# Value and key units in one block of every second round, the first key read between two clips

## What is computed

```python
lat = layer_norm(latents, ln_lat_g, ln_lat_b)      # latents: 4 x 256 x 128
ctx = layer_norm(context, ln_ctx_g, ln_ctx_b)      # context: 4 x 512 x 128
q = (lat @ Wq)                                     # 16 heads of 64
k, v = jnp.split(ctx @ Wkv, 2, axis=-1)
k = apply_rope(k, cos, sin)
attn = jnp.einsum('bhnd,bhsd->bhns', q, k) * scale
attn = jnp.clip(attn, -11.0, 11.0)
attn = jax.nn.softmax(attn, axis=-1)
out = jnp.einsum('bhns,bhsd->bhnd', attn, v)
return out @ Wo + bo
...
x = x + _L0_xattn_ref(_layernorm(x, axis=-1), ctx_1024, ...)
```

## Time and profile before

| | before |
|---|---|
| times | 425.7, 425.8 and 427.06 us, median 425.8 us |
| the profiled execution | 426.81 us, its span 424.9 us |
| PE busy | 402.7 us (95%) |
| DVE busy | 336.0 us (79%) |
| POOL busy | 257.5 us (61%) |
| ACT busy | 178.2 us (42%) |
| the rounds: S of round 0 to S of round 30 | 62.16 to 266.74 us |

### The profile page before, as it was taken

One profiled execution on the slowest core, in us unless ns is written; L12 is line 12 of the kernel. 1 busy time (PEld: TensorE's weight loads), 2 busy tenths in 40 slices (PEclk: granted clock), 3 DMA queues, 4 the chain that ended last, 5 costly groups with the idle time before them and its releaser, 6 DMA issues.

```text
span 424.9 us, 8269 instructions
## 1 busy us (share of the span) xinstructions
PE 402.7 (95%) x3040; PEld 296.0 (70%) x3040; DVE 336.0 (79%) x655; ACT 178.2 (42%) x282; POOL 257.5 (61%) x225
## 2 busy tenths in 40 slices
PE   3988799999999999999999998999999999999996
PEld 2666686667657776677766675687767788888884
DVE  8887759999989988998877997885778772655554
ACT  6867354545445245544263534336256443000000
POOL 6823549999998977998987686758335840000000
PEclk9999989999999999999999999999999999999999
DMA  7687422221211112111111162547347640000000
GB/s 181 160 214 105 89 66 61 52 81 44 51 44 32 38 37 52 26 45 43 40 37 39 41 110 65 137 69 153 54 107 155 148 64 2 6 13 8 6 6 14
DMA packets 84746, 28.63 MB, mean 67 GB/s; under 512 B 71957, under 2 KB 79050, under 8 KB 84706
## 3 DMA queue, kind: packets, MB, share of 16 engines
q1 hardware_dynamic: 81748, 26.80, 28.6%
q10 hardware_dynamic: 2958, 1.30, 1.4%
HBM read 17.67 MB, written 2.02 MB: 46 GB/s over the span
## 4 chain that ended last, share of the span: by engine, by line
PE 58%; DVE 31%; issue 4%; ACT 2%; DMA 2%; ACTq 1%; POOL 0%; DVEq 0%
PE psum L1230 7%; DVE rden L1638 7%; PE psum L1211 6%; DVE e_sb L1631 6%; PE psum L1414 5%; PE psum L1415 5%; PE psum L1413 5%; PE psum L1374 4%; PE psum L1376 4%; PE psum L1375 4%; PE psum L1249 3%; PE psum L1240 2%; DVE rope_b L1512 2%; DVE xn L1457 2%; DVE kT L1517 2%
## 5 line engine op out<-in xcount | busy, mean ns | idle before, releaser
L578 POOL TENSOR_TENSOR e_part<-e_sb 128x512 f32<-128x512 f32 x64 | 88.4, 1397 | 25.7 <-DVE e_sb L1631 25.7
L839 ACT ACTIVATE e_sb<-psum 128x1024 f32<-128x1024 f32 x64 | 62.3, 1023 | 81.4 <-PE psum L1211 78.5
L1631 DVE TENSOR_SCALAR e_sb<-e_sb 128x1024 f32<-128x1024 f32 x64 | 63.8, 1026 | 5.9 <-ACT e_sb L839 5.9
L1211 PE MATMUL psum<-q_t,kT 64*128 64x256 f32 x512 | 64.2, 389 | 0.0
L1230 PE MATMUL psum<-e_sb,v_sb 128*64 128x256 f32 x512 | 63.8, 386 | 0.0
L1638 DVE RECIPROCAL rden<-psum 128x256 f32<-128x256 f32 x32 | 55.9, 1747 | 9.1 <-PE psum L1240 9.1
L1840 DVE SCALAR_TENSOR_TENSOR x_sb<-psum,dw,x_sb 128x128 f32<-128x128 f32 x96 | 33.7, 351 | 37.1 <-PE psum L1415 34.5
L1211 PEld LDWEIGHTS psum<-q_t,kT 64*128 64x128 f32 x512 | 46.7, 186 | 13.9 <-issue 8.4
L1230 PEld LDWEIGHTS psum<-e_sb,v_sb 128*64 128x64 f32 x512 | 33.7, 136 | 22.3 <-issue 6.6
L607 POOL TENSOR_TENSOR xeT_lo<-xeT,xeT_hi 128x512 fp32r<-128x512 f32 x24 | 31.4, 1309 | 28.7 <-ACT xeT_hi L853 28.6
L570 POOL TENSOR_TENSOR kT<-kT,raw 128x512 f32<-128x512 f32 x32 | 44.2, 1382 | 2.7 <-DMA raw<-rope_b 1.9
(11 more groups left out here) (202 smaller groups left out, 733.3 us busy)
## 6 DMA issues: line engine op xcount, KB each, us to landing
raw<-rope_b SPq DMA_DIRECT2D x116, 64.0 KB, 2.0
w_raw<-in_L_ffn_W_dram SPq DMA_DIRECT2D x96, 64.0 KB, 2.3
gates<-gate_dram SPq DMA_DIRECT2D x6, 768.0 KB, 5.0
ctx_sb<-in_ctx_dram SPq DMA_DIRECT2D x4, 256.0 KB, 6.7
vbd<-v_dram SPq DMA_DIRECT2D x16, 52.6 KB
v_dram<-v_tok SPq DMA_DIRECT2D x4, 136.0 KB
raw<-in_L_xattn_Wkv_dram SPq DMA_DIRECT2D x2, 256.0 KB, 5.5
kT<-in_L_xattn_Wkv_dram SPq DMA_DIRECT2D x2, 256.0 KB, 4.8
```

The source lines that it names most:

```text
L578: pool.tensor_tensor(e_part[:, p % 2, half, :, :], e_sb[:, i % ERING, :, 0, :], e_sb[:, i % ERING, :, 1, :], ALU.add)\
L839: act.activation(e_sb[:, i % ERING, :, :, :].rearrange("p a k t -> p (a k t)"), psum[:, a:a + 2, :].rearrange("p a b -> p (a b)"), ACT.Exp ...
L1211: mm = pe.matmul(psum[:, 2 * (i % 2) + a, t * S:(t + 1) * S], key_slot(p)[rows, kt * P:(kt + 1) * P], q_t[rows, j % 2, p % 2, :], start=Tr ...
L1631: dve.tensor_scalar(e, e, E_LO, E_HI, ALU.max, ALU.min).then_inc(s["clip_done"], 1)
```

## The change

V and K of two rounds stand together in the even round: in TensorE's queue V, K, Q, V, K, and an odd round has only S, W and D there. On VectorE the first of the two key units is read between the two clips of the even round and the second behind them. The parts of `latents` are in other rounds (1, 2, 3 for sequence 1 where it was 0, 1, 2; 5, 6, 10 where it was 9, 10, 11; 11, 13, 16 where it was 14, 15, 16), the transposes of latents in rounds 4, 12, 18 (before 3, 12, 17); `context_lo` runs in rounds 8 and 17 (before 7 and 15), the first `output_bias` in round 4 (before 6). The waits count accordingly: `values_by(r)` is the number of value units that stand ahead of the end of round r.

```diff
@@ -286,10 +286,13 @@
         UNIT = [("k", n) for n in range(KC)] + [("v", 0), ("v", 1), ("k", KC), ("k", KC + 1), ("v", 2), ("v", 3)]
         UNIT_BANK = [7, 6, 7, 6, 7, 6, 7, 6, 7, 7]
         ROUND_VALUES = {}
-        for r in range(NPAIR):
-            if r + V_LEAD < NG * KC:
-                ROUND_VALUES[r] = len(UNIT)
-                UNIT.append(("v", r + V_LEAD))
+        for r in range(0, NPAIR - V_LEAD, 2):
+            ROUND_VALUES[r] = len(UNIT)
+            UNIT.extend([("v", r + V_LEAD), ("v", r + V_LEAD + 1)])
+
+        def values_by(r):
+
+            return min(r - r % 2 + V_LEAD + 2, NG * KC)
         UNIT_BANK += [5] * (len(UNIT) - len(UNIT_BANK))
 
         def bank_before(m):
@@ -299,10 +302,12 @@
                 n -= 1
             return n
 
-        LATENT_ROUNDS = {1: (0, 1, 2), 2: (9, 10, 11), 3: (14, 15, 16)}
+        LATENT_ROUNDS = {1: (1, 2, 3), 2: (5, 6, 10), 3: (11, 13, 16)}
+        LATENT_TURN = {4: 1, 12: 2, 18: 3}
+        CONTEXT_REST = {8: 2, 17: 3}
         CONTEXT_ROUND = {PPB - 2: 2, 2 * PPB - 2: 3}
         CONTEXT_NORM = {2: 2, PPB: 3}
-        extras = {rounds[2] + 1: ("latents", b) for b, rounds in LATENT_ROUNDS.items()}
+        extras = {r: ("latents", b) for r, b in LATENT_TURN.items()}
         for b in range(1, B):
             for t in range(TPB):
                 extras[b * PPB + 3 + 2 * t] = ("project", b - 1, t)
@@ -313,8 +318,8 @@
         for r in range(NPAIR):
             if r in CONTEXT_ROUND:
                 EXTRA.append(("context", CONTEXT_ROUND[r]))
-            if r + K_LEAD < NPAIR:
-                MISC.append(("keys", r + K_LEAD))
+            if r % 2 == 0 and r + K_LEAD < NPAIR:
+                MISC.extend([("keys", r + K_LEAD), ("keys", r + K_LEAD + 1)])
             if r in extras:
                 (EXTRA if r < NPAIR - K_LEAD else MISC).append(extras[r])
         MISC_NO = {what: n for n, what in enumerate(MISC)}
@@ -916,6 +921,8 @@
                     value_unit(ROUND_VALUES[r])
                 if r % 2 == 0 and r // 2 + 1 < NQ:
                     queries_out(r // 2 + 1)
+                if r in ROUND_VALUES:
+                    value_unit(ROUND_VALUES[r] + 1)
                 if r in CONTEXT_ROUND:
                     act.wait_ge(s["extra_ps"], EXTRA_NO["context", CONTEXT_ROUND[r]] + 1)
                     context_f(CONTEXT_ROUND[r])
@@ -1309,7 +1316,7 @@
 
             def route_1(i):
                 if i in ROUTE.values():
-                    pe.wait_ge(s["v_done"], min(i // 2 + V_LEAD, NG * KC - 1) + 1)
+                    pe.wait_ge(s["v_done"], values_by(i // 2))
                 if i == ROUTE["weights"]:
                     pe.wait_ge(s["ld_route"], 16 * (NR + 2))
                     pe.transpose(psum[:, 5, 0:DADDR], pw_sb[:, :], ident[0:DADDR, 0:DADDR])
@@ -1329,17 +1336,23 @@
                 if r == 0:
                     pe.wait_ge(s["x1_done"], NT)
                 if r in ROUND_VALUES:
+                    route_read(2 * r - 4)
                     route_read(2 * r - 2)
-                    if extra_before(r) > extra_before(r - 1):
+                    if extra_before(r) > extra_before(r - 2):
                         pe.wait_ge(s["extra_read"], extra_before(r))
                     unit(ROUND_VALUES[r])
-                if r + K_LEAD < NPAIR:
+                if r % 2 == 0 and r + K_LEAD < NPAIR:
                     misc_free(("keys", r + K_LEAD))
                     key_products(r + K_LEAD, bank(MISC_BANK)).then_inc(s["misc_ps"], 1)
                 if r % 2 == 0 and r // 2 + 1 < NQ:
                     queries(r // 2 + 1)
+                if r in ROUND_VALUES:
+                    unit(ROUND_VALUES[r] + 1)
+                if r % 2 == 0 and r + K_LEAD < NPAIR:
+                    misc_free(("keys", r + K_LEAD + 1))
+                    key_products(r + K_LEAD + 1, bank(MISC_BANK)).then_inc(s["misc_ps"], 1)
                 if r in CONTEXT_ROUND:
-                    pe.wait_ge(s["v_done"], r + V_LEAD + 1)
+                    pe.wait_ge(s["v_done"], values_by(r))
                     turn_context(CONTEXT_ROUND[r], EXTRA_BANK, "extra_ps")
                 weigh_values(2 * r)
                 route_1(2 * r)
@@ -1349,7 +1362,9 @@
                 if r in extras:
                     what = extras[r]
                     if what in EXTRA_NO:
-                        pe.wait_ge(s["v_done"], r + V_LEAD + 1)
+                        pe.wait_ge(s["v_done"], values_by(r))
+                        if EXTRA_NO[what]:
+                            pe.wait_ge(s["extra_read"], EXTRA_NO[what])
                     else:
                         misc_free(what)
                     if what[0] == "latents":
@@ -1753,7 +1768,7 @@
             local_residual(3)
             context_lo(1)
 
-            beside = {6: (output_bias, 0), NPAIR - 6: (output_bias, 1)}
+            beside = {4: (output_bias, 0), NPAIR - 6: (output_bias, 1)}
 
             def route_1(i):
                 for stage in ROUTE:
@@ -1772,13 +1787,15 @@
                         latents(b, rounds.index(r))
                 if r + 1 < NPAIR:
                     clip(2 * r + 2)
+                    if r % 2 == 0 and r + K_LEAD < NPAIR:
+                        key_unit(r + K_LEAD, MISC_BANK)
                     clip(2 * r + 3)
-                if r + K_LEAD < NPAIR:
-                    key_unit(r + K_LEAD, MISC_BANK)
+                if r % 2 == 0 and r + K_LEAD < NPAIR:
+                    key_unit(r + K_LEAD + 1, MISC_BANK)
                 if r == NORM_ROUND:
                     final_norm(0, 1)
-                if r - 1 in CONTEXT_ROUND:
-                    context_lo(CONTEXT_ROUND[r - 1])
+                if r in CONTEXT_REST:
+                    context_lo(CONTEXT_REST[r])
                 if r in beside:
                     work, arg = beside[r]
                     work(arg)
```

## The result

The changed kernel took 434.26 us in the median (433.17 to 435.07, 4 runs), the kernel before, in runs of the same series, 425.93: a ratio of 1.0178, with a 95% interval of 1.0142 to 1.0213. It is slower by 1.8%, some 8 us. The profiled execution of the changed kernel took 435.07 us with a span of 433.2, that of before 426.81 with 424.9, so the two traces differ by 8.3 us. From S of round 0 to S of round 28 there are 191.01 us before and 199.69 after: 8.68 us more, so the whole loss lies in these rounds.

The account below looks back on a forecast made before the run. TensorE was taken to set the pace in the rounds, with VectorE's lateness as second bound. The terms -2.9 + 2.4 + 9.8 - 3.5 = +5.8 us gave 431.6 us for the median, range 422 to 436.

Parts of the forecast that it names:

- slower as the likeliest: All slower outcomes together, chance 0.60: losses at the second K win 0.48, GpSimd as the bound 0.12.
- wrong under 4: Sign: if TensorE's idle time in front of the second key unit is under 4 us in all, the forecast is wrong.
- The saved entries and exits: TensorE's order: fewer entries into and exits from fp32r matmuls, 0.21 us for each of 14 pairs, 2.9 us less.
- The second key unit in ordinary rounds: Second K waits for VectorE's read of the first: 0.3 us in each of eight even rounds, 2.4 us more.
- The latents parts: Latents work on VectorE ahead of the first key read delays the second K in rounds 2, 6, 10, 16, 18: 9.8 us.
- no term is made of the clock: The granted clock was 1.00 in the rounds profiled before, so the forecast counted no clock loss.
- round 6 was to start late by about 1 us: VectorE's extra work ahead of round 6 makes its start late by about 1 us, so that round loses 3.5.
- What goes: TensorE's old waits from VectorE's lateness, in four even rounds (2, 8, 12, 16), go: 3.5 us less.
- GpSimd as the bound: Rival: D and the exponents wait for GpSimd's sums, +3 us, about 429; chance 0.12.
- Faster, since the clips get free: Rival: with the key read between clips, the second finds GpSimd done and VectorE gains time; 421.7 to 422.9 us, chance 0.26.
- the sign that the prediction named for this rival: Faster rival's sign: even-round clips all near 0.7 us and VectorE idle ahead of each key read.
- as was said against this rival: Against the faster rival: VectorE's regained time lies behind the first key read, but the second K hangs on what lies ahead.

## Why the prediction was right, point by point

It said 431.6 us in a range of 422 to 436, with slower as the likeliest. It is 434.26, slower. The mechanism was the right one: in the rounds TensorE stands 9.7 us in front of the second key unit, where the prediction would have been wrong under 4. But it had 5.8 us and 8.3 came, so a third of the loss is missing from its sum, and two of its terms were too small.

**The saved entries and exits, 2.9 us: right.** Odd rounds without a projection are 4.24 us from S to S (4.23 was said), the units of the block follow each other at 0.81, 0.69 and 0.72.

**The second key unit in ordinary rounds, 2.4 us: a little low.** Seven of the eight even rounds named there last 8.07 to 8.33 us after their added transposes and projections are taken off, so they lose 0.16 to 0.42 against 7.91, as taken. Round 0 loses 1.13 and was wrongly put among them: four additions to x_sb (1.00 us from 62.34) and a `context_lo` (0.94) of the stage before stand in front of its first clip on VectorE, and this clip takes 1.79, beside a GpSimd sum (63.84 to 65.47). Together 3.1.

**The latents parts, 9.8 us: right in kind, low in size.** Rounds 2, 6, 10, 16 and 18 lose 2.97, 4.60, 1.80, 1.79 and 0.78, together 11.9, where 2.6, 3.5, 1.1, 1.1 and 1.5 were taken. Of the difference of 2.1 some 1.6 are no idle time at all but the low clock behind the wait of round 6: W and D there take 3.68 us to the next S (112.01 to 115.69), where round 2 takes 2.31 (83.30 to 85.61), and the context transposes in front of them 0.79, where round 14 takes 0.53. The prediction said that no term is made of the clock, because the granted clock was 1.00 in the rounds before. That held for waits of up to 1.3 us, the longest that the rounds before had; the change made longer ones. This is the step that failed. That the rest of the term fits is in part luck: round 6 was to start late by about 1 us, but its division begins 0.23 behind S (102.88 against 102.65), and round 18 was taken too high as well; rounds 10 and 16, where the normalizations take 2.41 and 2.01, were taken too low by about as much.

**What goes, 3.5 us: right, as far as it can be read.** The sum -2.9 + 3.1 + 11.9 - x has to give 8.68, so x is 3.4; this closes the sum and measures nothing by itself. What the timeline shows is that the four old waits, in front of Q in rounds 2, 8 and 16 and of V in round 12, are gone.

**GpSimd as the bound: no.** Nothing in TensorE's timeline of these rounds waits for GpSimd's sums, and GpSimd waits more for the clips (36.4 us in all, 25.7 before). It has a part in the loss all the same, as the prediction had it: the latents parts that stand ahead of the read are long because its sums run beside them (2.48 in round 2, above).

**Faster, since the clips get free: no.** This is the group of the clips in the changed kernel:

```profile
L1646 DVE TENSOR_SCALAR e_sb<-e_sb 128x1024 f32<-128x1024 f32 x64 | 61.8, 979 | 7.5 <-ACT e_sb L844 7.5
```

They take 979 ns in the mean, where 1026 were before, so VectorE did gain 3 us of its own work. But in the 13 even rounds with key reads the first clip takes 1.00 us in the mean and the second 1.16 (0.91 and 1.34 before), and not near 0.7, the sign that the prediction named for this rival. What is gained in the even rounds lies behind the first read, and TensorE hangs on what lies ahead of it, as was said against this rival; and by itself the read between the clips frees nothing (429.02).

**What was not seen** is how much the block hangs on the table of latents rounds: with the old one it costs 8 us more.

## What to carry to other kernels

Two units through one PSUM bank in one block turn a read that had a whole round of slack into a link of the chain: before putting them together, play the reader's queue from the start of the block to that read, with everything that stands ahead of it. Moving the producer earlier does nothing if the next reuse of a bank then waits (K V Q V K moved the stall of the ordinary rounds from K to V), and moving other work behind the read pays back half, because the reading engine's lateness is lost at its next consumers. A saving of 0.2 us per pair of rounds is too small to put such a link at risk. A second key unit with a bank of its own, which would take the link away, was not run.

## What the hardware showed that was not expected

TensorE's granted clock fell behind some of its waits to 0.50, which is the 1.2 GHz level, for some microseconds; a window that holds a stretch at either level shows a mean. The rows are windows: length, busy times as above, granted clock third from the end. First the changed kernel, the wait of round 6 and what came behind it, then its wait of 1.64 us in round 28:

```profile
107.60:110.42 2.82, 0.04 (x1) 0.00 (x0) 2.79 (x8) 0.60 (x1) 2.74 (x4) 1.00 0.09 23
110.42:112.01 1.59, 1.59 (x7) 1.08 (x8) 1.59 (x2) 0.00 (x0) 0.96 (x2) 0.82 0.47 117
112.01:115.17 3.16, 3.16 (x19) 1.86 (x19) 1.04 (x2) 1.41 (x2) 3.08 (x3) 0.55 0.03 8
115.17:115.69 0.52, 0.52 (x6) 0.14 (x2) 0.00 (x0) 0.00 (x0) 0.52 (x1) 1.00 0.00 0
...
263.15:264.79 1.64, 0.00 (x1) 0.03 (x1) 1.61 (x4) 1.12 (x2) 1.64 (x2) 1.00 0.63 100
264.79:268.66 3.87, 3.87 (x30) 2.27 (x30) 1.96 (x4) 1.19 (x3) 3.16 (x4) 1.00 0.00 0
```

Then the same wait of round 28 in the kernel with the second key unit behind half of W, and the wait of round 2 in the kernel with the order K V Q V K:

```profile
259.76:261.43 1.67, 0.00 (x0) 0.03 (x1) 1.64 (x4) 1.12 (x2) 1.67 (x2) 1.00 0.54 86
261.43:264.91 3.48, 3.48 (x18) 1.75 (x18) 1.29 (x3) 0.60 (x1) 2.85 (x3) 0.67 0.00 0
```

```profile
80.80:83.23 2.43, 0.02 (x2) 0.01 (x1) 2.40 (x6) 2.13 (x5) 2.35 (x4) 1.00 0.12 30
83.23:85.00 1.77, 1.77 (x5) 0.92 (x7) 1.69 (x2) 0.00 (x0) 1.14 (x2) 0.57 0.45 112
```

A wait of 1.64 us was followed by 1.00 in one kernel, one of 1.67 by 0.67 in another; 2.66 by 1.00, 2.41 and 2.70 by the low level; in the rounds a fall came only with a wait or behind one, and not behind each. What decides stays open. The kernel before has a fall too, in the stage ahead of its rounds:

```profile
52.60:56.00 3.40, 3.40 (x34) 2.82 (x36) 1.60 (x7) 1.83 (x5) 1.51 (x2) 0.50 0.39 97
```

So each of the two traces has one such fall, and this is not what sets them 8.3 us apart, though the 8.68 us of the rounds hold the fall of round 6. In the four runs of the changed kernel the mean clock was 0.995, 0.995, 0.991 and 1.000 at 435.07, 433.62, 434.91 and 433.17 us: the one without a fall is the shortest, by 0.5 to 1.9 us. Even that one is 7 us above the median of the kernel before, so the clock is a small part of the result.
